# Attention probabilities kept in PSUM and turned by crossbar DMAs in place of TensorE transposes, in a Perceiver layer on one Trainium2 core

## The reference

```python
q = (x @ Wq).reshape(B, N, HEADS, DIM_HEAD).transpose(0, 2, 1, 3)
k = (context @ Wk).reshape(B, M, HEADS, DIM_HEAD).transpose(0, 2, 1, 3)
v = (context @ Wv).reshape(B, M, HEADS, DIM_HEAD).transpose(0, 2, 1, 3)
dots = jnp.einsum('bhnd,bhmd->bhnm', q, k) * SCALE
attn = jax.nn.softmax(dots, axis=-1)
out = jnp.einsum('bhnm,bhmd->bhnd', attn, v)
return out.transpose(0, 2, 1, 3).reshape(B, N, HEADS * DIM_HEAD) @ Wo + bo
```

## Time and profile before

| | us |
|---|---|
| median of 3 runs | 1026.83 |
| lowest and highest run | 1025.34, 1029.33 |
| the profiled execution's own time | 1028.92 |
| its span in the trace | 1027.0 |
| busy in the span: PE, DVE, ACT, POOL | 870.6, 831.1, 684.0, 774.3 |

### The profile page before, as it was taken

The page is one execution under the profiler, slowest core; times in us unless marked ns, Lnnn a source line. Parts: engine busy times, 40 slices in busy tenths (PEclk is TensorE's granted clock), DMA queues, the critical chain, the costliest instruction groups (busy, mean ns, idle before and its releaser), DMA issues.

```text
span 1027.0 us, 29818 instructions
## 1 busy us (share of the span) xinstructions
PE 870.6 (85%) x8554; PEld 720.6 (70%) x8554; DVE 831.1 (81%) x2343; ACT 684.0 (67%) x2029; POOL 774.3 (75%) x1237
## 2 busy tenths in 40 slices
PE   7989998999999999999999999999998461049895
PEld 7777786878787887878787887887776261036664
DVE  5899888989999989899999999998988657025563
ACT  3777776778777778778777777777775113037774
POOL 5788888898989898888889898989886503735554
PEclk9999999999999999999999999999999655559998
DMA  9111111111111111111111211111100840111120
GB/s 233 33 33 33 32 33 33 33 33 36 49 42 32 31 31 31 31 31 31 31 31 32 59 33 31 31 31 31 31 2 2 129 162 14 52 43 53 47 54 17
DMA packets 56836, 45.11 MB, mean 44 GB/s; under 512 B 8367, under 2 KB 54578, under 8 KB 56769
## 3 DMA queue, kind: packets, MB, share of 16 engines
q1 hardware_dynamic: 54464, 40.01, 15.9%
q0 software_dynamic: 2304, 4.25, 1.3%
HBM read 37.25 MB, written 7.52 MB: 44 GB/s over the span
## 4 chain that ended last, share of the span: by engine, by line
PE 36%; POOL 31%; issue 13%; DVE 12%; ACT 4%; DMA 1%; POOLq 1%; DVEq 1%; ACTq 0%; SPq 0%
POOL Pn L925 10%; PE bank L396 6%; PE bank L373 6%; PE bank L420 4%; POOL cT L916 4%; PE bank L1369 3%; PE bank L413 3%; PE bank L385 3%; POOL sorted_rows L1232 3%; POOL chi L906 2%; PE bank L1384 2%; DVE cs L839 2%; DVE nmax L783 2%; POOL clo L910 2%; DVE Tl L777 1%
## 5 line engine op out<-in xcount | busy, mean ns | idle before, releaser
L925 POOL TENSOR_TENSOR Pn<-Pe,rsum 128x1028 f32<-128x1028 f32 x128 | 243.1, 1899 | 74.4 <-DVE rsum L798 74.4
L713 ACT ACTIVATE Pe<-bank,nmax 128x257 f32<-128x257 f32 x512 | 240.5, 475 | 30.1 <-DVE nmax L783 29.5
L783 DVE TENSOR_REDUCE nmax<-bank 128x1 f32<-128x257 f32 x512 | 202.0, 415 | 35.3 <-PE bank L373 34.0
L373 PE MATMUL bank<-cT,qh 96*128 96x257 f16 x1024 | 184.8, 275 | 21.1 <-ACT Pe L713 19.6
L777 DVE TENSOR_TENSOR Tl<-bank,Th 128x512 f16<-128x512 f32 x256 | 173.8, 680 | 0.5 <-ACT Th L702 0.4
L702 ACT ACTIVATE Th<-bank 128x512 f16<-128x512 f32 x256 | 141.3, 595 | 48.5 <-PE bank L420 48.5
L420 PE MATMUL bank<-identf,Pn 128*128 128x128 f32 x1024 | 149.3, 274 | 0.0
L373 PE MATMUL bank<-cT,ql 96*128 96x257 f16 x512 | 139.2, 272 | 0.0
L420 PEld LDWEIGHTS bank<-identf,Pn 128*128 128x128 f32 x1024 | 115.1, 142 | 6.1
L373 PEld LDWEIGHTS bank<-cT,qh 96*128 96x128 f16 x1024 | 90.3, 97 | 38.3 <-issue 15.9
L713 ACT ACTIVATION_READ_ACCUMULATOR Pe<-bank,nmax 128x1 f32 x512 | 103.8, 203 | 0.0
(11 more groups left out here) (213 smaller groups left out, 2444.4 us busy)
## 6 DMA issues: line engine op xcount, KB each, us to landing
rawT<-in_dram SPq DMA_DIRECT2D x32, 385.5 KB, 3.9
raw<-in_dram SPq DMA_DIRECT2D x32, 384.0 KB, 4.4
sorted_rows<-fill SPq DMA_DIRECT2D x1, 2620.0 KB, 21.1
xs<-sorted_rows SPq DMA_DIRECT2D x40, 65.5 KB, 1.8
R<-in_dram SPq DMA_DIRECT2D x4, 512.0 KB, 5.9
Z<-last_rows SPq DMA_DIRECT2D x128, 2.2 KB
w1r<-in_dram SPq DMA_DIRECT2D x4, 512.0 KB, 13.7
w2fr<-in_dram SPq DMA_DIRECT2D x4, 512.0 KB, 14.2
```

The costliest lines, as they stand in the source:

```text
L373: last = nc.tensor.matmul(bank[SB[t]][:, 0:M], w[:, par, b, t * P:(t + 1) * P], cT[:, s4, c, 0:M], start=(k == 0), stop=(k == 2))
L713: nc.scalar.activation(Pe[:, n_par(j + 1), t, :], bank[SB[t]][:, 0:M], ACT.Exp, bias=nmax[:, n_par(j + 1), t:t + 1], accum_out=sums[:, n_p ...
L783: nc.vector.tensor_reduce(nmax[:, n_par(j + 1), t:t + 1], bank[SB[t]][:, 0:M], AX.X, ALU.max, negate=True).then_inc(s_nmax, 1)
L925: nc.gpsimd.tensor_tensor(Pn[:, par, :, :], Pe[:, par, :, :], rsum[:, par, :].unsqueeze(2).broadcast_to([P, QT, M]), ALU.mult)\
```

## The change

The scores of all four tiles stand in four banks of their own, declared as one tensor `quad` [128, 4, 512]. The maxima are taken over two tiles at once. The exponentials are written back in place, in fp32 and without the accumulated sum. For each pair of tiles ACT copies the high half (`Pmain[..., 0, :]`) to SBUF, DVE makes the low half from PSUM, and two tiny copies and a tiny subtraction split the last column into `Plast`. One DMA with `transpose=True` on SP's queue turns the 20 blocks of 128 x 128 fp16 of a sequence (PHL to PT). The probabilities are not normalised: the context halves get a column of ones (`CW` = 97), so the values product, which now has the turned probabilities as weights and the context as the moving operand, gives the key sum as its 97th column; DVE takes its reciprocal and scales the output (On). ACT and POOL split On, and a second DMA turns its 8 blocks (Ohl to OT), from which the output product reads its weights with a stride of four elements. It now accumulates over four steps in PSUM, so the residual add comes once in four steps. ACT makes chi in place of POOL. The query columns are ordered by token, then head. The mixing block runs one step later (`mixed`) and uses bank 6, the queries bank 4. Z is loaded once. The unrolled start has five rounds in place of four, the pipeline one step more.

The core of the diff (removed functions stand above; in the new ones a few removed lines are left out):

```diff
-        bank = [top.enter_context(nc.psum_tensor(f"bank{i}", [P, 512], F32)) for i in range(8)]
+        quad = top.enter_context(nc.psum_tensor("quad", [P, 4, 512], F32))
+        bank = [quad[:, i, :] for i in range(4)]
+        bank += [top.enter_context(nc.psum_tensor(f"bank{i}", [P, 512], F32)) for i in range(4, 8)]
...
+        CW = CC + 1
+        CS = CC + 2
+        chi = asb("chi", [P, NC8, MC, CS], F16)
+        clo = asb("clo", [P, NC8, MC, CS], F16)
...
+        MK = MC * P
+        PHL = asb("PHL", [P, NP2, QT * (2 * MK + P)], F16)
+        Pmain = PHL[:, :, 0:QT * 2 * MK].rearrange("p n (t l k) -> p n t l k", t=QT, l=2)
+        Plast = PHL[:, :, QT * 2 * MK:].rearrange("p n (t i) -> p n t i", t=QT)
+        PT = asb("PT", [P, NP2, QT * (2 * MC + 1), P], F16)
+        On = asb("On", [P, NP2, QT, CC])
+        Ohl = asb("Ohl", [P, NP2, 2, QT, P], F16)
...
+        OT = asb("OT", [P, NP2, 2 * QT, GB, P], F16)
...
-        def pe_scores(n, par, b, s4, tiles):
+        def pe_scores(n, par, b, s4):
             wait(nc.tensor, s_cTh, n + 1)
             wait(nc.tensor, s_cT, n + 1)
-            for t in tiles:
-                wait(nc.tensor, s_exp, QT * n + 1 if t == 3 else QT * (n - 1) + (t or 3) + 1)
-                for k, (w, c) in enumerate(((qh, 0), (qh, 1), (ql, 0))):
-                    last = nc.tensor.matmul(bank[SB[t]][:, 0:M], w[:, par, b, t * P:(t + 1) * P],
-                                            cT[:, s4, c, 0:M], start=(k == 0), stop=(k == 2))
+            for k, t in enumerate(ORDER):
+                if k == 0:
+                    wait(nc.tensor, s_Pm, n)
+                if k == 2:
+                    wait(nc.tensor, s_Pl, n)
+                for i, (w, c) in enumerate(((qh, 0), (qh, 1), (ql, 0))):
+                    last = nc.tensor.matmul(bank[t][:, 0:MP], w[:, par, b, t * P:(t + 1) * P],
+                                            cT[:, s4, c, 0:MP], start=(i == 0), stop=(i == 2))
                 last.then_inc(s_S, 1)
...
+        O5 = bank[5][:, 0:QT * CW].rearrange("p (t c) -> p t c", c=CW)
+        def pe_pv(n, par, s8, turns):
+            wait(nc.tensor, s_clo, n + 1)
+            wait(nc.tensor, s_PT[par], 16 * turns)
+            if n_static(n) == 0:
+                wait(nc.tensor, s_pad, 6)
+                wait(nc.tensor, s_z, 16)
+            wait(nc.tensor, s_On, n)
...
             for t in range(QT):
+                for k, (hl, w) in enumerate(((0, chi), (0, clo), (1, chi))):
+                    for c in range(MC):
+                        nc.tensor.matmul(O5[:, t, :], PT[:, par, (2 * t + hl) * MC + c, :], w[:, s8, c, 0:CW],
+                                         start=(k == 0 and c == 0), stop=False)
+                z = Z[:, bass.ds(n, 1), 0:CW].rearrange("p o c -> p (o c)")
+                last = nc.tensor.matmul(O5[:, t, :], PT[0:R3, par, QT * 2 * MC + t, :], z, start=False, stop=True)
             last.then_inc(s_PV, 1)
...
+        def pe_y(n, part, gp, turns):
+            if part == 0:
+                for b in range(GB):
+                    wait(nc.tensor, s_OT[GB * gp + b], 16 * turns)
+                wait(nc.tensor, s_res, turns * 2 - 2 + gp)
+            if n_static(n) == 6:
                 wait(nc.tensor, s_abl, 8)
             for h in range(part * QT, part * QT + QT):
+                for k, (hl, w) in enumerate(((0, Bhi), (0, Blo), (1, Bhi))):
+                    o = OT[0:CC, gp, hl * QT + h // QT, :, :].rearrange("p b r -> p (b r)")[:, h % QT:GB * P:QT]
+                    last = nc.tensor.matmul(bank[7][:, 0:C], o, w[:, h, :],
+                                            start=(h == 0 and k == 0), stop=(h == H - 1 and k == 2))
             last.then_inc(s_y, 1)
...
         def pe_step(it, j):
             n, g, jj, gp = where(it, j)
             if exists(n + 1):
                 if (j + 1) % GB == 0:
                     wait(nc.tensor, s_ql, n + 5)
-                pe_scores(n + 1, ((j + 1) // GB) % NP2, (j + 1) % GB, (j + 1) % 4, (0, 1, 2))
+                pe_scores(n + 1, ((j + 1) // GB) % NP2, (j + 1) % GB, (j + 1) % 4)
+            if exists(n - 1):
+                pe_pv(n - 1, (j - 1) % NP2, (j - 1) % NC8, 4 * it + (j - 1) // 2 + 1)
             if exists(n + 5):
-                pe_mix_free(it, j)
                 pe_q(n + 5, (j + 1) % GB, bass.ds(P * (g + 1 + (jj + 1) // GB), P))
-            if exists(n + 1):
-                pe_scores(n + 1, ((j + 1) // GB) % NP2, (j + 1) % GB, (j + 1) % 4, (3,))
-            if exists(n - 1):
-                pe_pv(n - 1, (j - 1) % NP2, (j - 1) % NC8, ((j - 1) // GB) % NP2, (j - 1) % GB,
-                      it + 1 + (j - 1) // NC8)
-            if exists(n - 5):
-                if jj == 1:
-                    wait(nc.tensor, s_Ol, GB * g)
-                wait(nc.tensor, s_L12, n if n_static(n) is None else min(n, B))
-                pe_y(n, (jj + 3) % GB, gp if jj == 0 else 1 - gp)
-            if exists(n):
-                wait(nc.tensor, s_elo, n + 1)
-                wait(nc.tensor, s_L12, n)
-                nc.tensor.transpose(bankh[7][:, 0:P], e12p[:, n_par(j), :], ident[:, :]).then_inc(s_left, 1)
-                wait(nc.tensor, s_pn, n + 1)
-                pe_probsT(n, n_par(j), 0)
+            if exists(n - 6):
+                part = (jj - 2) % GB
+                m = (j - 6 - part) // GB
+                pe_y(n, part, m % 2, it + m // 2 + 1)
             pe_mix(it, j, n)
...
         def act_step(it, j):
             n, g, jj, gp = where(it, j)
+            if exists(n + 4):
+                par, first = ((j + 4) // GB) % NP2, (j + 4) % GB == 0
+                turns = it + 1 + ((j + 4) // GB - ((j + 4) // GB) % NP2) // NP2
+                if first:
+                    wait(nc.scalar, s_ctx[par], 16 * turns)
+                act_chi(n + 4, (j + 4) % NC8, par, (j + 4) % GB)
+                if first:
+                    wait(nc.scalar, s_ctxT[par], 16 * turns)
+                act_cT(n + 4, (j + 4) % 4, par, (j + 4) % GB)
+            if exists(n + 1):
+                p = n_par(j + 1)
+                for k, t in enumerate(ORDER):
+                    if k % 2 == 0:
+                        wait(nc.scalar, s_nmax, 2 * (n + 1) + k // 2 + 1)
+                    nc.scalar.activation(bank[t][:, 0:MP], bank[t][:, 0:MP], ACT.Exp, bias=nmax[:, p, t:t + 1]).then_inc(s_exp, 1)
+                    if k == 1:
+                        wait(nc.scalar, s_PT[p], 16 * (4 * it + (j + 1) // 2))
+                    if k % 2:
+                        src = quad[:, t - 1:t + 1, 0:MK]
+                        wait(nc.scalar, s_exp, QT * (n + 1) + k + 1)
+                        nc.scalar.activation(Pmain[:, p, t - 1:t + 1, 0, :], src, ACT.Copy).then_inc(s_Ph, 1)
+            if exists(n + 5):
+                act_q(n + 5, (gp + 1 + (jj + 1) // GB) % NP2, (j + 1) % GB)
             if exists(n - 1):
+                p = n_par(j - 1)
+                wait(nc.scalar, s_OT[(j - 3) % 8], 16 * (it + (j - 3) // 8 + 1))
+                wait(nc.scalar, s_On, n)
+                nc.scalar.activation(Ohl[:, p, 0, :, 0:CC], On[:, p, :, :], ACT.Copy).then_inc(s_Oh, 1)
+            act_mix(*mixed(it, j))
             act_early(n)
+        def act_chi(n, s8, par, b):
+            wait(nc.scalar, s_PV, n - 7)
+            nc.scalar.activation(chi[:, s8, :, 0:CC], raw[:, par, b, :, :], ACT.Copy).then_inc(s_chi, 1)
...
+        def dve_max(n, p, pair):
+            wait(nc.vector, s_S, QT * n + 2 * pair + 2)
+            t = ORDER[2 * pair]
+            nc.vector.tensor_reduce(nmax[:, p, t:t + 2], quad[:, t:t + 2, 0:M], AX.X, ALU.max, negate=True)\
+                .then_inc(s_nmax, 1)
+        def dve_low(n, p, pair, s_h, s_l):
+            t = ORDER[2 * pair]
+            wait(nc.vector, s_Ph, 2 * n + pair + 1)
+            nc.vector.tensor_copy(Plast[:, p, t:t + 2, 0:2], quad[:, t:t + 2, MK:MP]).then_inc(s_h, 1)
+            nc.vector.tensor_tensor(Pmain[:, p, t:t + 2, 1, :], quad[:, t:t + 2, 0:MK], Pmain[:, p, t:t + 2, 0, :], ALU.subtract)
+            wait(nc.vector, s_h, n + 1)
+            nc.vector.tensor_tensor(Plast[:, p, t:t + 2, 2:3], quad[:, t:t + 2, MK:M], Plast[:, p, t:t + 2, 0:1],
+                                    ALU.subtract).then_inc(s_l, 1)
...
         def dve_step(it, j):
             n, g, jj, gp = where(it, j)
+            if exists(n + 1):
+                dve_max(n + 1, n_par(j + 1), 0)
+            dve_stat_waits(it, j, g, jj)
+            if exists(n + 1):
+                dve_max(n + 1, n_par(j + 1), 1)
             dve_stat(it, j, g, jj, gp)
+            dve_mix_a(*mixed(it, j))
+            if exists(n + 1):
+                dve_low(n + 1, n_par(j + 1), 0, s_hm, s_Pm)
+            if jj == 2 and exists(g - 2, G):
                 wait(nc.vector, s_m["stat"], g - 1)
+            if exists(n - 1):
+                p = n_par(j - 1)
+                wait(nc.vector, s_Oh, n - 2)
+                wait(nc.vector, s_Ol, n - 2)
+                wait(nc.vector, s_PV, n)
```

(50 more changed lines are left out.)

333 lines of the change are left out of this document (91 added, 242 removed).

## The result

The changed kernel takes **1204.07 us** (median of 4 runs, 1202.57 to 1204.98), the kernel before 1027.13 us beside it (1025.34 to 1029.33): 1.172 times as long, 95% interval 1.1693 to 1.1747. The forecast was 1012 us, with a range from 970 to 1200.

The account below looks back on a forecast made before the run. DVE was taken as the bound. Step: 6.10 - 0.06 - 0.37 + 0.45 - 0.17 = 5.95 us, times 128 -19 us, plus 4 us for the extra step: 1013.9 from 1028.9, median 2.1 lower, 1012 us; range 970 to 1200.

Parts of the forecast that it names:

- ql 0.60: DVE's own work: the subtraction for the query low half, 512 columns, priced at 0.60 us a step before and after.
- 4.03 us: Sum of DVE's own listed work in a step after the change, against 4.09 us before: 0.06 us less.
- no more than before: ACT's work a step, 4.58 us before: exponentials lose accumulator reads, chi comes with 192 columns, so no increase.
- scores of tiles 2 and 3 may start as soon as the first low is done: TensorE's scores come early enough that DVE's old waits of 0.37 us a step mostly go.
- rival (d): TensorE falls out of its full clock as its gaps grow: over 1200 us, chance 0.03.
- my largest rival at 0.36: Rival (a): crossbar DMAs become the bound by rate, SP issue or landing; slower than before, chance 0.36, over half below 1200.
- 256 B cost some 18 ns: Crossbar DMA price per 256 B source row: 224 rows an engine, 4.7 us a step with the context, hidden.
- point of decision: Crossbar row price at which turning would fill the forecast step: (5.95 - 0.7)/224 = 23 ns a row.
- some 6 to 7 us: Landing time of the crossbar's big turn, 655 KB, with PE's 2 us of slack taking a small overrun.
- The new wait: DVE's first low subtraction waits for maximum, exponentials and ACT copy: 0.45 us a step on the mean, ends 0.2 and 0.9.
- 0.15 us a step: Whole forecast gain in the pipeline's step, from 6.10 to 5.95 us; times 128 is -19 us.
- the term for contention (-0.17): DVE's fp32 SBUF work speeds up as POOL works less: 0.17 us a step off, ends 0 and 0.3.

Follow-up runs that it names:

- experiment 6: The kernel before with only the query halves written strided, fp16 elements 8 bytes apart: 1109.13 us, ratio 1.0787.
- experiment 2: The changed kernel with tiles in order 0, 1, 2, 3 and the boundary's wait for ql split by pair of tiles: 1152.59 us, ratio 1.1212.
- experiment 11: experiment 3 with the next query quarter's matmuls, high half and low half moved earlier on TensorE, ACT and DVE: 1043.58 us, ratio 1.0118.
- experiment 5: The changed kernel with 24 idle matmuls ahead of TensorE's wait for ql at each group boundary: 1149.6 us, ratio 1.1177.
- experiment 4: The changed kernel with both crossbar DMAs turning one block in place of 20 and 8, the others constant: 1208.64 us, ratio 1.1755.
- experiment 7: experiment 3 with both crossbar DMAs turning one block in place of 20 and 8: 1047.45 us, ratio 1.0188.
- experiment 3: The changed kernel with the edits of experiment 1 and experiment 2 together: 1052.35 us, ratio 1.0223.
- experiment 1: The changed kernel with the query halves written contiguously and PSUM read with the stride instead: 1099.03 us, ratio 1.0675.

## Why the prediction was wrong

**The step that failed first: "ql 0.60" in DVE's own work.** I priced the query halves by their shape, and took them over unchanged. The diff of `q_view` stood in my own description as "ordered by token, then head", and I didn't ask what it does to an instruction: same operation, same columns, but the fp16 elements are written 8 bytes apart. It doubles both halves (586 to 1312 and 676 to 1299 ns), 0.62 us more a step on DVE, the engine I had named as the bound. By my own rule that is 128 x 0.62 = 79 us, and experiment 6 measures 82. The sum's "4.03 us" of own work should have been 4.65. I also counted ACT as having "no more than before", while it has 0.73 us more.

**The second: scores taken as always in time.** I wrote that "scores of tiles 2 and 3 may start as soon as the first low is done". Ahead of them stands the boundary's wait for all four quarters of the next group, and the changed order asks for tile 3, made of the newest quarter, in the first pair. The old kernel has the same wait, with nothing to pay for it; the change takes the slack away. The wait measures 51 us together with its share of the clock (experiment 2). Where the slack went is shown by experiment 11: with the queries earlier in the lists of all three engines, TensorE waits for ql no more.

**The third: rival (d) had the right mechanism, with too small a chance and without its trigger.** "0.77 busy I expect it to hold" argued from an average over 500 us. The granted clock doesn't fall in the average, it falls behind a gap of 3.1 us in an otherwise full row of work. 54 us by experiment 5, against a chance of 0.03. That the columns at half clock then lie on the path (the scores and the values product) I had seen: "4.6 us of columns are 9".

**The crossbar, my largest rival at 0.36, was none.** PE hardly waiting for PT is what the forecast said, and experiments 4 and 7 show the turns hidden in the steady stretch. But the price was too low, and the share of 0.80, within the 0.6 to 0.8 that I gave, is luck: it holds at a step of 7.33 us, and at the step that I had forecast it is 0.95 (experiment 3). "256 B cost some 18 ns" went wrong by drawing a line through two mean packets of other sizes; a row takes 23 ns (experiment 4), so the turns are 224 x 23 ns = 5.2 us a step and 5.9 with the context, in place of 4.7 (by the share in experiment 3, 0.95 x 5.96 = 5.7 us). That is just my "point of decision". By this estimate a step much shorter than 5.7 us would have met the crossbar. The landing of the big turn, "some 6 to 7 us", is 5.0. The Trainium skill, "VectorE: DVE Perf Modes", section "The three transpose paths", has 1309 ns for one 128x128 block. 20 blocks landing in 5.0 us, 0.25 each, show that it is no price per block in a long turn, as I had read it; one block alone lands in 2.2 us here.

**The range.** 1204 lies just above its upper end. That it is so near is chance: the end was drawn for the crossbar, and none of the three costs above is in it.

**What held.** DVE's prices by spacing, in its timeline above: low subtraction 0.60 (609.65 to 610.25), key sum 0.21 forecast 0.20, On 0.48 forecast 0.46, the small ones 0.06 to 0.08 forecast 0.08. The new wait, 0.39 for 0.45 (in experiment 3; in the changed kernel itself the same row has 17.0 us, 0.25 a step). POOL at 220.7 us over 500/7.33 = 68 steps is 3.2 us a step, as said.

**What of the 0.15 us a step remains when both flaws are out.** Experiment 11 has DVE at 5.91 us a step in place of 5.92, so the forecast's own gain is nearly all missing as well. DVE's waits are as long as before (22.8 us for the copies, 7.5 for the scores and 1.0 for the values product, 0.37 us a step). What failed is the term for contention (-0.17), by these rows of it (against 286, 932, 788 and 527 ns before for the scan, num, denm and den):

```profile
L827 DVE TENSOR_TENSOR_SCAN cs<-onesn,fab 128x32 f32<-128x32 f32 x176 | 52.6, 358 | 0.0
...
L866 DVE SCALAR_TENSOR_TENSOR denm<-den,er 128x256 f32<-128x256 f32 x10 | 11.4, 1138 | 0.0
...
L851 DVE SCALAR_TENSOR_TENSOR den<-esum,nlw,sst 128x256 f32<-128x256 f32 x11 | 9.3, 843 | 0.0
...
L861 DVE SCALAR_TENSOR_TENSOR num<-ekv,nlw,sst 128x256 f32<-128x256 f32 x10 | 4.8, 476 | 0.0
```

num is at 476 ns as forecast, while the scans, denm and den became slower, though POOL is busy only 0.55 of the time. Summed by the means of these and of scl and sst, the mixing operations are 0.15 us a step dearer than before; in the changed kernel itself (scans 246 ns, denm 418) they are 0.19 cheaper, close to the forecast. The crossbar is not what slows them: with one block turned (experiment 7, share 0.18) scan and denm take 311 and 1138 ns, with all of them (experiment 3, share 0.95) 304 and 1136. Nor does POOL's work in all decide: in experiment 6 it is the same in every step as before, and num takes 578 ns in place of 932, denm 410 in place of 788. I take it that what stands beside an operation decides, but this is not shown: which of POOL's operations that is, I didn't try.

Eight steps being equal, the 12 us that experiment 11 still takes more lie outside them. Its first On starts at 35.4 us, 2.3 before Ol; the fifth is 1.1 us ahead, the 17th, at 144.9 us, 8.4 behind, the 121st still 8.4, the last, at 803.5 us, 10.5, and 2.9 us come behind it. So most of it is lost between 60 and 145 us, with the clock at 0.92 from 60 to 150 (0.98 before). The cause of that stretch was not separated; a part of the difference can be the chip, on which the kernel before took 1031.8 us, where its trace is one of 1028.9.

**A count that was off without harm.** The "82 steps in 500 us, so 6.10 us each" rested on the number of maxima. The distance of the Ol rows gives 5.92. No record is missing (the whole trace has 512 maxima): the last maximum of the pipeline starts at 782.7 us, so the 82 steps fill 483 us of the window and not 500. The sum used only differences, so the 1012 hardly changes by it; the step that the crossbar had to stay below was 0.2 us shorter than I reckoned.

## What to carry to other kernels

Price an instruction whose access pattern the diff changes as a new instruction, even where its shape is the old one; a layout that saves a strided read of weights elsewhere can be bought with a loop order that writes contiguously and strides through PSUM, for nothing. When a change takes slack away, list the waits that cost nothing before, those at group boundaries too, and ask which of the things waited for is the newest. Look at the granted clock behind TensorE's regular gaps and not at its mean busy share alone, and test what it costs with idle matmuls in the gap.

## What the runs showed of the hardware

- **Stride of a 2-byte write.** 96x512 fp16 from fp32 in PSUM to SBUF: contiguous 587 ns on ACT and 673 on DVE; elements 8 bytes apart 1310 to 1313 and 1296 to 1301 (the changed kernel and experiments 2, 5 and 6). The PSUM side read with elements 512 bytes apart costs nothing (experiment 1). The Trainium skill, "SBUF — State Buffer", section "Door 1: The DMA port swizzle", says that two hits in a line of 16 bytes keep the full rate, up to a stride of 8 elements of 2 bytes. At a stride of four elements these writes do not follow it; the measurement decides.
- **The crossbar.** 20 blocks of 128x128 fp16 from SBUF to SBUF land in 5.0 us, 8 in 3.1, one in 2.2 (experiment 4). A row of 256 B takes 23 ns of a DMA engine. From 300 to 800 us the waits for its outputs are 0.2 us at a DMA share of 0.95 (experiment 3) and 2.4 us at 0.96 (experiment 11).
- **TensorE's clock.** 1.00 up to and in a gap of 3.1 us, 0.50 from 616 to 622 us, then up again; 0.99 where the gap was filled with matmuls, whose results nobody reads.
- **Weights with a stride.** The output product's weights, read four elements apart, cost no time between matmuls: at 609.17, 609.23 and 609.28 us its matmuls start 0.056 us apart, as the queries' do.
